# One exponential over all four score banks per step in an attention and feed-forward kernel

## What is computed

```python
q, k, v = (split_heads(x @ W.T + b) for W, b in ((Wq, bq), (Wk, bk), (Wv, bv)))
scores = einsum('hbnd,hbmd->hbnm', k, q) / 16
out = einsum('hbnm,hbmd->hbnd', softmax(scores), v)      # heads merged again
x = layernorm(x + out @ Wo.T + bo)
gate, up = x @ wg.T, x @ wu.T                            # hidden width 768, int weights / 127
x = layernorm(x + (silu(gate) * up) @ wd.T)
```

## Time and profile before

| | |
|---|---|
| median of 3 runs | 2877.07 us (2870.65 to 2880.16) |
| the profiled execution, its own time | 2875.62 us |
| its span, first to last instruction | 2873.8 us |
| granted TensorE clock, mean | 0.982 |
| PE busy | 2688.1 us, 94% |
| ACT busy | 2133.8 us, 74% |
| DVE busy | 1363.5 us, 47% |
| POOL busy | 539.2 us, 19% |

### The profile page before, as it was taken

The page is one execution under the profiler, slowest core; times in us unless marked ns, Lnnn a source line. Parts: engine busy times, 40 slices in busy tenths (PEclk is TensorE's granted clock), DMA queues, the critical chain, the costliest instruction groups (busy, mean ns, idle before and its releaser), DMA issues. The chain is left out here.

```text
span 2873.8 us, 47670 instructions
## 1 busy us (share of the span) xinstructions
PE 2688.1 (94%) x17592; PEld 985.2 (34%) x17592; DVE 1363.5 (47%) x2845; ACT 2133.8 (74%) x2369; POOL 539.2 (19%) x544
## 2 busy tenths in 40 slices
PE   5689999999999999999999999999999999999996
PEld 3223233332333333243333333333233332333333
DVE  4313554455454545545444454545544454454437
ACT  0587777777777777777777777777877777777881
POOL 1001111121121212211121111212211121111113
PEclk7899999999999999999999999999999999999998
DMA  3111121021210212021021211202121021211100
GB/s 119 46 46 57 38 68 43 23 82 30 72 46 30 73 31 81 29 67 53 20 83 30 67 44 42 68 24 79 31 67 49 17 89 29 66 46 38 32 16 37
DMA packets 80081, 144.13 MB, mean 50 GB/s; under 512 B 27584, under 2 KB 30272, under 8 KB 75584
## 3 DMA queue, kind: packets, MB, share of 16 engines
q1 hardware_dynamic: 79808, 140.46, 15.7%
HBM read 88.48 MB, written 50.33 MB: 48 GB/s over the span
## 5 line engine op out<-in xcount | busy, mean ns | idle before, releaser
L556 ACT ACTIVATE probs<-psum 128x1024 f32<-128x1024 f32 x2048 | 1994.0, 1025 | 632.2 <-PE psum L927 631.4
L927 PE MATMUL psum<-probs,v 128*32 128x512 f32 x8192 | 992.2, 602 | 0.0
L927 PE MATMUL psum<-kstack,qstack 51*128 51x512 f16 x4096 | 678.7, 385 | 84.7 <-ACT probs L556 61.5
L927 PEld LDWEIGHTS psum<-kstack,qstack 51*128 51x128 f16 x4096 | 146.2, 93 | 825.7 <-ACT probs L556 456.4
L927 PEld LDWEIGHTS psum<-probs,v 128*32 128x32 f32 x8192 | 214.8, 109 | 516.7 <-issue 512.5
L466 POOL TENSOR_TENSOR ffn<-h,ffn 128x512 f16<-128x512 f32 x192 | 221.4, 1155 | 688.3 <-DVE ffn L718 586.9
L445 POOL TENSOR_TENSOR squares<-parts 128x512 bf16<-128x512 f16 x128 | 133.0, 1039 | 689.6 <-DVE parts L660 689.6
L669 DVE SCALAR_TENSOR_TENSOR tanh_out<-tanh_out,psum 128x512 f32<-128x512 f32 x192 | 130.6, 680 | 224.8 <-ACT tanh_out L537 224.4
L794 DVE STREAM_TRANSPOSE flipped<-psum 128x512 f32<-128x512 f32 x128 | 91.7, 716 | 296.9 <-PE psum L927 296.7
L660 DVE SCALAR_TENSOR_TENSOR parts<-psum,scales,parts 128x512 f16<-128x512 f32 x128 | 95.5, 746 | 285.7 <-ACT parts L528 285.7
L927 PE MATMUL psum<-ffn,upT 128*128 128x512 f16 x768 | 213.5, 381 | 4.1 <-DVE tanh_out L669 3.5
(11 more groups left out here) (95 smaller groups left out, 1613.6 us busy)
## 6 DMA issues: line engine op xcount, KB each, us to landing
parts_dram<-parts SPq DMA_DIRECT2D x64, 512.0 KB, 2.8
qstack<-parts_dram SPq DMA_DIRECT2D x384, 64.0 KB, 2.2
kstack<-parts_dram SPq DMA_DIRECT2D x384, 64.0 KB, 2.1
x_pre<-in_L_attn_x SPq DMA_DIRECT2D x17, 1024.0 KB, 4.9
x_res<-in_L_attn_x SPq DMA_DIRECT2D x16, 1024.0 KB, 5.3
out<-x_res SPq DMA_DIRECT2D x32, 512.0 KB, 2.7
kstack<-shift_parts SPq DMA_DIRECT2D x384, 4.0 KB, 1.7
ffn<-in_L_ffn_w_gate SPq DMA_DIRECT2D x1, 768.0 KB, 8.9
```

The source lines that it names most:

```text
L556: nc.scalar.activation(probs[:, (STEPS * b + k) % SLOTS, 2 * pr:2 * pr + 2, :], scores[pr], ACT.Exp, scale=score_scale[par]).then_inc(prob ...
L927: return nc.tensor.matmul(o, lhsT, rhs, start=start, stop=stop)
```

## The change

The four score banks become one unit. ACT runs one ACTIVATE of 128 x 2048 a step in place of two of 128 x 1024. PE waits once, before the first of the four score matmuls, for the exponential of the whole step before, and signals `scores_ready` once, with the fourth. Both semaphores now count steps, not pairs, so SP's waits are rescaled and release at the same points. The extras of a step, for `h` 0 and 1, come behind the one exponential.

```diff
-UNITS = 2 * STEPS
+UNITS = STEPS
-        scores = [psum[:, 2 * s:2 * s + 2, :] for s in range(2)]
+        scores = psum[:, 0:GROUP, :]
...
-                    for pr in range(2):
-                        act.wait_ge(scores_ready, UNITS * b + 2 * k + pr + 1)
-                        if pr == 0 and (k >= SLOTS or not first):
-
-                            act.wait_ge(pv_done, STEPS * b + k - SLOTS + 1)
-                        nc.scalar.activation(probs[:, (STEPS * b + k) % SLOTS, 2 * pr:2 * pr + 2, :], scores[pr], ACT.Exp,
-                                             scale=score_scale[par]).then_inc(probs_ready, 1)
-                        extras(k, pr)
+                    act.wait_ge(scores_ready, UNITS * b + k + 1)
+                    if k >= SLOTS or not first:
+
+                        act.wait_ge(pv_done, STEPS * b + k - SLOTS + 1)
+                    nc.scalar.activation(probs[:, (STEPS * b + k) % SLOTS, :, :], scores, ACT.Exp,
+                                         scale=score_scale[par]).then_inc(probs_ready, 1)
+                    for h in range(2):
+                        extras(k, h)
...
+                if k or not first:
+
+                    pe.wait_ge(probs_ready, UNITS * b + k)
                 for pr in range(2):
-                    if k or not first:
-
-                        pe.wait_ge(probs_ready, UNITS * b + 2 * k + pr - 1)
                     for half in range(2):
                         at = ROW_TILE * half
-                        ins = mm(scores[pr][:, half, :], qstack[at:at + STACK, g % 2, pr, t * P:(t + 1) * P],
+                        ins = mm(scores[:, 2 * pr + half, :], qstack[at:at + STACK, g % 2, pr, t * P:(t + 1) * P],
                                  kstack[at:at + STACK, g % 2, pr, hf * HALF:(hf + 1) * HALF], True, True)
-                    ins.then_inc(scores_ready, 1)
+                ins.then_inc(scores_ready, 1)
...
-                pe.wait_ge(probs_ready, UNITS * b + 2 * k + 2)
+                pe.wait_ge(probs_ready, UNITS * b + k + 1)
```

More of the change, by code:

```diff
@@ L365, in batch @@
                     store_parts(b + 1, 0)
-                sp.wait_ge(scores_ready, UNITS * b + 2 * PER_GROUP)
+                sp.wait_ge(scores_ready, UNITS * b + PER_GROUP)
                 load_stack(b, 2)
@@ L374, in batch @@
                 load_shift(b, 2)
-                sp.wait_ge(scores_ready, UNITS * b + 4 * PER_GROUP)
+                sp.wait_ge(scores_ready, UNITS * b + 2 * PER_GROUP)
                 load_stack(b, 3)
@@ L382, in batch @@
                 if not last:
-                    sp.wait_ge(scores_ready, UNITS * b + 6 * PER_GROUP)
+                    sp.wait_ge(scores_ready, UNITS * b + 3 * PER_GROUP)
                     for s in range(2):
```

## The result

The changed kernel takes 2947.05 us in the median of four runs (2942.94 to 2956.88), against 2874.41 us before (four runs, 2870.65 to 2880.16). The ratio is 1.0256 with a 95% interval of 1.0223 to 1.0289, so it is slower by 2.6%, some 73 us. The forecast was 2937 us, 2903 to 2983. The profiled execution has a span of 2942.8 us, 69.0 us over that of before.

What follows compares the result with a forecast made beforehand. PE was taken to bound the middle batches, ACT batches 0 and 15. Middle batches +2, batches 0 and 15 +35 and late drains +25 gave +62 us on 2875.6 us: 2937 us, range 2903 to 2983.

Steps and rivals of the forecast that it cites:

- The loop: Every step: scores, hand-over to ACT, exponential and hand-over back run in series, so no step is under 2.58 us.
- Even steps: 14 middle batches: each of 32 even steps goes from 2.39 to 2.58 us, +6.1 us a batch.
- late second pairs: Odd steps of middle batches: second score pairs delayed by extras between the exponentials; their stalls go, -7.0 us a batch.
- Short odd steps: Middle batches: eight odd steps then shorter than the loop are filled up to it, +1.1 us a batch.
- Late drains: Odd steps 21, 27, 39, 41, 43: PE waits for banks drained late behind extras, 1.8 us a batch, +25 us.
- 5 x 0.37: Late drains of a middle batch: five odd steps, each priced at step 27's 0.37 us wait, 1.8 us.
- Batches 0 and 15: First and last batch, ACT-bound before: every step at least 2.58 us, +17.4 and +17.3 us, together +35 us.
- the clock: Batch 0's light steps: PE idling drops the granted clock to 0.50, about 1 us each; ten falls, +10 us.
- The wait at step 55: PE's wait for POOL in step 55: left at nothing, at most 0.8 us a batch or 11 us to gain.
- the longer: Rival on the exponential: it costs nearly two halves, 1.94 us, loop 2.64 us, 2983 us; chance 0.10.
- the much shorter one: Rival, faster: short exponential, at the lower bound 1.71 us, loop 2.41 us, -50 us, 2826 us; chance 0.06.
- the rival of 2.70 us a loop: Skill's ACTIVATE budget: exponential 2.00 us, loop 2.70 us, some 3035 us; set aside for the rows, no chance given.

Runs made afterwards that it cites:

- e1: Changed kernel's order of waits, but two exponentials of 128 x 1024 a step in place of one of 128 x 2048; 2977.38 us, ratio 1.0380.
- e5: e3 with one more ACTIVATE of 128 x 128 behind each exponential, into a buffer nothing reads; 3021.35 us, ratio 1.0542.
- e8: e4 with the first pair of scores waiting for both exponentials of the step before; 2823.51 us, ratio 0.9860.
- e4: Kernel before, with the extras ahead of the first exponential of their step in place of between the two; 2797.62 us, ratio 0.9757.
- e3: Changed kernel with the extras of a step ahead of its exponential in place of behind it; 2894.74 us, ratio 1.0097.
- e9: Kernel before, two exponentials and overlap kept, with the extras behind the second half in place of between the two; 2837.81 us, ratio 0.9884.
- e10: e4 with POOL's reduction of the maximum of x for the batch after next moved from step 46 to step 23; 2749.54 us, ratio 0.9579.

## Why the prediction was right

**The loop.** Forecast 0.61 + 0.04 + 1.88 + 0.06, 2.58 us with the third digit; measured 0.61, 0.03, 1.88 and 0.06 us, 2.58. The length of the exponential over four banks, which no row of before had, was the largest unknown. The slope between the sizes measured gave 1.88, and the trace has 1.878. e1, e5 and e8 moved the loop to 2.64, 2.75 and 2.43 us, and even steps followed each time.

**Even steps, stalls and short odd steps.** The even steps rose by 0.19 us (by 5.8 us a batch, forecast 6.1, since step 56 was long before), and the late second pairs of 7.0 us a batch went. Not all of that was gained: e4 takes away every late pair, and its steps 33 and 41 take 3.12 and 3.31 us as before, since they wait for a drain there. So 6.4 of the 7.0 us could be won. Short odd steps are filled up: steps 5, 7, 11, 17, 23, 49 and 61 all take 2.58 us. What the sum said, that the gain in odd steps pays for the loss in even ones, was right: in e3, where the drains are early, a middle batch without steps 55 and 56 takes 0.1 us more than before.

**Late drains.** The mechanism was right, and so were four of the five places. The size was a little low: 1.8 us a batch forecast, 2.1 measured. In the term "5 x 0.37" the price and the count were both off, and partly made up for each other: against e3 the steps cost 0.55 (21), 0.39 (27), 0.24 (39) and 0.89 us (43, where both banks of two `tanh` were wanted). Step 41 costs nothing; it takes 3.13 us in the changed kernel and in e3. The wait in it, in the changed kernel and then in e3:

```profile
899.51 0.72 DVE L794 STREAM_TRANSPOSE flipped<-psum 128x512 f32<-128x512 f32 x1 [2.85 <-PE psum L927]
...
900.86 1.04 PE L927 MATMUL psum<-ffn,upT 128*128 128x512 f16 x4 [0.37 <-DVE tanh_out L669]
```
```profile
885.82 0.72 DVE L794 STREAM_TRANSPOSE flipped<-psum 128x512 f32<-128x512 f32 x1 [5.41 <-PE psum L927]
...
886.46 0.65 DVE L669 SCALAR_TENSOR_TENSOR tanh_out<-tanh_out,psum 128x512 f32<-128x512 f32 x1
...
887.16 1.04 PE L927 MATMUL psum<-ffn,upT 128*128 128x512 f16 x4 [0.37 <-DVE tanh_out L669]
```

In both the drain of `tanh` stands in DVE's queue behind a transpose that waits for the products, so it makes no difference when `tanh` ran. Another 0.09 us comes in each of steps 15 and 31, which I had not seen. A middle batch took 2.3 us more than before, forecast 2.0.

**Batches 0 and 15.** +17.3 us for batch 15, and it was 17.6. Batch 0 took 20.0 us more than before, 2.6 more than forecast. The mechanism named for it, the clock, did occur. The timeline of PE in the changed kernel, and a window with its clock (the 0.50):

```profile
117.55 0.61 PE L927 MATMUL psum<-kstack,qstack 51*128 51x512 f16 x4 [1.97 <-ACT probs L555]
118.09 3.53 PE L927 MATMUL psum<-probs,v 128*32 128x512 f32 x16
```
```profile
118.30:121.70 3.40, 3.40 (x18) 0.56 (x12) 0.04 (x1) 1.77 (x1) 0.00 (x0) 0.50 0.02 5
```

Behind an idle of 1.97 us PE ran at 1.2 GHz for the time of one group of products, which took 3.53 in place of 1.92 us. Behind the first steps it happened once in batch 0, not ten times. The step took 4.00 us in place of 2.58, so 1.4 us of the 2.6 are this. Steps 0 to 2, 2.7 us over the loop where I had put 2, give 0.7, and five steps of 2.67 us the rest.

**The wait at step 55.** I left it at nothing, and in the total it was nothing (PE waits for POOL 26.3 us, before 25.1). So this term came out by luck: nothing was the sum of two opposite effects, longer steps ahead of it and later drains at the start of POOL's chain, as e3 (9.3 us, with early drains) and e9 (42.7 us, with late ones and short steps) show.

**The rivals.** The exponential saves the 0.06 us a step that its length promised, so neither the longer nor the much shorter one held; at 1.88 us the loop is far from the 2.49 us from which the change would pay. The rule of the Trainium skill ("Perfetto Trace Analysis", section "Optimizing Scalar/DVE Operations") that grouping into larger operations can raise throughput is put there for a saturated engine, with about 51 ns of access overhead on PSUM; the trace agrees in size (0.06 us an instruction), but ACT was busy 71% of the span, and what the saving gave was a shorter loop (2.58 in place of 2.64 us in e1). The time went to the overlap that it takes. The budget of the Trainium skill ("ScalarE: Activation LUTs", section "Rules for kernel authors") gives 2.00 us for this ACTIVATE as an estimate, and the trace has 1.88; the page gives that budget for an ACTIVATE whose bias is a pointer operand, and this one has none, so the rival of 2.70 us a loop applied it to a case that it doesn't name.

## What to carry to other kernels

Buffers that are filled and read in two halves by two engines are a double buffer; making them one unit puts filling, reading and both hand-overs in series, and the step can't be shorter than their sum. Work that sum out from the rows (here 2.58 us) and compare it with the time in which the bounding engine does a step (here 2.39 us) before saving instructions on an engine that has idle time. And look at where small operations stand in an in-order queue: the time in which that engine waits for its main input anyway is free, and moving eight `hi` and twelve `tanh` a batch there gained 2.4% with no other change.

## What was not expected of the hardware

Behind steps 15 and 31 of the changed kernel the next scores also wait for two groups of DMAs, the last of them issued 7 us before (825.10 us in batch 4), and these steps take 2.67 us in place of 2.58: in batch 4 the scores of step 16 start 0.15 us behind ACT's end (831.95 to 832.10), those of step 1 0.06. e3 shows 2.67 there too, and e5 2.84 in place of 2.75. What causes it was not tried. POOL's two reductions, 0.4 us of recorded work each, hold its queue for 27.7 us (e4, from 857.65 to 885.36 us). With one of the two moved away (e10), step 55 takes 2.61 us in every batch.
